# A deformable stage whose sampling products are packed into five matmuls of up to 126 rows

## The chip, the core and the metric

One core of one Trainium2 chip runs the whole program: two layers of a network on 64 images of 1024 channels and 14 by 14 pixels, in fp32. The metric is the device time of one execution in microseconds.

## What is computed

The first layer is a bottleneck of three convolutions (1x1, 3x3, 1x1) with batch norm. The second layer, which the change touches, is a bottleneck whose 3x3 convolution is deformable:

```python
out = relu(group_norm(conv(x, w1)))                  # 1024 -> 256 channels
om = conv(out, w_off, pad=1) + b_off                 # 27 channels
off_x, off_y, mask = om[:, :9], om[:, 9:18], sigmoid(om[:, 18:])
py, px = grid_y + off_y, grid_x + off_x              # a place for each of 9 taps and 196 pixels
sampled = bilinear_sample(out, py, px) * mask        # four corners, zero outside the image
out = relu(group_norm(einsum('bckhw,ock->bohw', sampled, w2)))
out = relu(group_norm(conv(out, w3)) + x)
```

Bilinear sampling is written as a matmul over the 196 source pixels: the sample at (py, px) is the sum over pixels (q, r) of out(q, r) times relu(1 - |py - q|) times relu(1 - |px - r|). The two factors are called hats here, one along y and one along x.

## The kernel before

The first layer takes the first third of the span and is the same in both kernels. The second layer goes over 32 pairs of images. Every product in nearly fp32 precision is three fp32r matmuls (`product3`, lines 69 to 74): high part by high part, and the two mixed terms of high and low.

**Units and tiles.** A pair has nine units of sampling weights: units 0 to 7 are two taps of one image (2 x 196 = 392 columns), unit 8 is the last tap of both images. Each unit serves two tiles of 128 channels, but unit 8 four tiles of 196 columns: 20 tiles a pair (`sample_tile`, line 2015). The 196 source pixels lie on partitions in two halves of 98 = 7 rows of the image by 14 pixels. A tile is therefore 2 halves x 3 terms = 6 matmuls of 98 rows. Its sum is split by ScalarE (`part_v`, high part) and VectorE (`rest_v`, low part, line 1801), and `deform_part` multiplies it by the weights of the taps.

**How a unit is made.** The hats of a pair are made by ScalarE as 126 rows (9 taps x 14 places), the y hats are multiplied by the mask on GpSimd (`mask_hats`, line 1662), and all are stored to DRAM (`store_hats`, line 1321, four DMAs). `load_hats` (lines 1291 to 1314) reads them back, spread over partitions, by three DMAs of 98 rows of 1568 bytes: y hats of the upper seven image rows, each row of the source repeated for 14 partitions; y hats of the lower seven rows likewise; x hats, the 14 rows repeated seven times. The source of each has an outer dimension of 7 and an inner one of 14. GpSimd multiplies y hats by x hats (`make_s`, line 1655), ScalarE takes the high part (`part_s`, line 1438), VectorE the low part (`rest_s`, line 1793). There is a ring of `HATS` = 3 slots; the loads of unit u wait for the low part of unit u - 3 (`s_lo_made`), after which the slot is free.

**What sets the order.** Each engine has one queue, written out by hand as a list of steps in `step`. Work of five pairs is interleaved in it. All loads and stores of hats and the loads of `x1` are issued by SyncE (SP) in one queue; ScalarE's queue issues the loads of `y_in` (line 1364) and the stores of the outputs (line 1354). On SyncE the order of a pair is: loads of units 4 to 8 with the two loads of `x1` among them, the four stores of the next pair's hats, loads of units 0 to 3 of that pair. On GpSimd `mask_hats` of the next pair stands behind `make_s` of unit 8.

**TensorE** runs, for each pair, 20 tiles of `sample_tile`, 36 parts of three matmuls in `deform_part`, 1x1 convolutions (`conv1`, `conv3`, 48 matmuls each), `offsets` (18), three selections (`spread_offsets`, line 1999) and eight transposes of the activations (`transposes`, line 2010).

## Time and profile before

| | us |
|---|---|
| median of three runs | 2997.18 |
| lowest and highest | 2995.97, 2997.70 |
| profiled execution, its own time | 2997.73 |
| its span | 2995.6 |
| first layer and change-over, about | 1000 |
| TensorE busy in the span | 2936.5 (98%) |
| VectorE | 2374.3 (79%) |
| ScalarE | 1798.1 (60%) |
| GpSimd | 717.0 (24%) |

TensorE's clock was granted at full rate in 0.993 of the span. The figures of busy time are averages over stages; what matters below is the steady stretch of the second layer, roughly 1100 to 2900 us. Matmuls overlap their neighbours in the records, so that the distance between two starts, and not the mean duration, is what one costs.

### The profile page before, as it was taken

The numbers are of one execution on the slowest core, as the hardware profiler recorded it, in microseconds if no ns is written. First come the engines' busy times: TensorE is split into PE (matmuls) and PEld (weight loads), VectorE is DVE, ScalarE is ACT, GpSimd is POOL, SyncE is SP. The second block draws the span as 40 slices with busy tenths as digits, with TensorE's granted clock in tenths as the row PEclk, the third lists the DMA queues.
The fourth block names the chain that finished last, engine by engine and source line by source line (L and its number), as shares of the span: only waits on it lengthen the run. The fifth ranks groups of instructions, "written<-read, shape, count | busy, mean of one in ns | idle before, by whom it ended". The sixth has DMA issues, their size and how long they took to land.

```text
span 2995.6 us, 46528 instructions
## 1 busy us (share of the span) xinstructions
PE 2936.5 (98%) x16518; PEld 2861.0 (96%) x16518; DVE 2374.3 (79%) x4872; ACT 1798.1 (60%) x3281; POOL 717.0 (24%) x433
## 2 busy tenths in 40 slices
PE   9999999999998999999999999999999999999997
PEld 9999999999997999999999999999999999999997
DVE  5755888965665688888888888888888888888875
ACT  4544332246654566676666766667666676666664
POOL 0000000000001333333333333333333333333331
PEclk9999999999999999999999999999999999999998
DMA  7774111035653354444444444444444444444431
GB/s 270 217 232 128 44 44 44 22 127 221 256 214 115 119 163 145 145 153 147 157 146 148 155 149 148 151 150 146 155 150 152 152 141 148 148 160 148 143 113 73
DMA packets 209175, 437.34 MB, mean 146 GB/s; under 512 B 18640, under 2 KB 170160, under 8 KB 203312
## 3 DMA queue, kind: packets, MB, share of 16 engines
q1 hardware_dynamic: 159376, 326.77, 32.4%
q10 hardware_dynamic: 49568, 107.60, 11.2%
q8 instruction: 131, 2.15, 0.3%
q14 instruction: 100, 0.82, 0.1%
HBM read 307.66 MB, written 126.64 MB: 145 GB/s over the span
## 4 chain that ended last, share of the span: by engine, by line
PE 58%; DVE 9%; ACT 1%; issue 0%; DMA 0%; POOL 0%; ACTq 0%; DVEq 0%; POOLq 0%
PE work L72 7%; PE work L74 7%; PE sample L72 6%; PE work L73 6%; PE deform L72 6%; PE sample L74 6%; PE sample L73 6%; PE deform L73 6%; PE deform L74 6%; DVE s_lo L1793 2%; DVE x L1817 2%; DVE x_lo L1705 1%; DVE v_lo L1801 1%; DVE x L1699 1%; PE work L2010 1%; PE work L1999 1%
## 5 line engine op out<-in xcount | busy, mean ns | idle before, releaser
L1655 POOL TENSOR_TENSOR hats<-hats 98x784 f32<-98x784 f32 x288 | 602.6, 2092 | 887.2 <-DMA hats<-hat_scratch 857.4
L1447 ACT ACTIVATE v_hi<-sample 128x392 fp32r<-128x392 f32 (+1 forms) x640 | 295.5, 462 | 337.5 <-PE sample L74 318.8
L72 PE MATMUL sample<-s_hi,aT_hi 98*128 98x392 f32 (+1 forms) x1280 | 426.6, 333 | 18.4 <-DVE s_lo L1793 13.5
L73 PE MATMUL sample<-s_lo,aT_hi 98*128 98x392 f32 (+1 forms) x1280 | 419.6, 328 | 0.0
L74 PE MATMUL sample<-s_hi,aT_lo 98*128 98x392 f32 (+1 forms) x1280 | 419.3, 328 | 0.0
L72 PE MATMUL deform<-v_hi,w_w 128*128 128x392 f32 x1152 | 406.4, 353 | 0.9 <-DVE v_lo L1801 0.7
L73 PE MATMUL deform<-v_lo,w_w 128*128 128x392 f32 x1152 | 392.7, 341 | 0.0
L74 PE MATMUL deform<-v_hi,w_w 128*128 128x392 f32 x1152 | 391.6, 340 | 0.0
L1801 DVE TENSOR_TENSOR v_lo<-sample,v_hi 128x392 fp32r<-128x392 f32 (+1 forms) x640 | 327.1, 518 | 74.6 <-ACT v_hi L1447 73.0
L1793 DVE TENSOR_TENSOR s_lo<-hats,s_hi 98x784 fp32r<-98x784 f32 x288 | 346.6, 1204 | 2.6 <-ACT s_hi L1438 1.6
L1438 ACT ACTIVATE s_hi<-hats 98x784 fp32r<-98x784 f32 x288 | 245.6, 853 | 104.3 <-DVE x L1699 77.4
L72 PEld LDWEIGHTS sample<-s_hi,aT_hi 98*128 98x128 f32 x1280 | 241.4, 189 | 34.7 <-DVE s_lo L1793 21.1
L73 PEld LDWEIGHTS sample<-s_lo,aT_hi 98*128 98x128 f32 x1280 | 242.6, 190 | 0.0
L74 PEld LDWEIGHTS sample<-s_hi,aT_lo 98*128 98x128 f32 x1280 | 241.9, 189 | 0.0
L72 PEld LDWEIGHTS deform<-v_hi,w_w 128*128 128x128 f32 x1152 | 217.0, 188 | 8.3 <-issue 5.8
L1817 DVE SCALAR_TENSOR_TENSOR x<-y_home,gn,x 128x196 f32<-128x196 f32 x496 | 220.5, 505 | 0.1
L288 POOL TENSOR_TENSOR bn<-bn,half_neg 128x2 f32<-128x2 f32 (+1 forms) x3 | 3.0, 1012 | 904.8 <-DVE bn L307 622.1
L73 PEld LDWEIGHTS deform<-v_lo,w_w 128*128 128x128 f32 x1152 | 217.4, 189 | 0.0
L74 PEld LDWEIGHTS deform<-v_hi,w_w 128*128 128x128 f32 x1152 | 216.6, 188 | 0.0
L1705 DVE TENSOR_TENSOR x_lo<-x,x_hi 128x392 fp32r<-128x392 f32 x256 | 199.9, 781 | 9.8 <-ACT x_hi L1379 9.8
L1699 DVE SCALAR_TENSOR_TENSOR x<-in_home,scale,x 128x392 f32<-128x392 f32 x248 | 196.2, 792 | 6.2 <-DMA in_home<-y_scratch 6.1
L1503 ACT ACTIVATE x<-x,gn 128x196 f32<-128x196 f32 x496 | 191.6, 448 | 0.7 <-DVE x L1817 0.4
(226 smaller groups left out, 7349.0 us busy)
## 6 DMA issues: line engine op xcount, KB each, us to landing
hats<-hat_scratch SPq DMA_DIRECT2D x768, 150.1 KB
x<-in_x SPq DMA_DIRECT2D x64, 784.0 KB, 5.9
in_home<-y_scratch ACTq DMA_DIRECT2D x248, 196.0 KB, 2.9
out<-x ACTq DMA_DIRECT2D x62, 784.0 KB, 3.4
y_home<-in_x SPq DMA_DIRECT2D x32, 784.0 KB, 5.0
y_scratch<-y_out SPq DMA_DIRECT2D x16, 1568.0 KB, 5.9
terms<-in_x SPq DMA_DIRECT2D x30, 784.0 KB, 4.7
y_scratch<-y_home SPq DMA_DIRECT2D x15, 1568.0 KB, 5.2
```

What stands on the lines that cost most here:

```text
L72: nc.tensor.matmul(out, w_hi, x_hi, start=start, stop=False)
L73: nc.tensor.matmul(out, w_hi, x_lo, start=False, stop=False)
L74: return nc.tensor.matmul(out, w_lo, x_hi, start=False, stop=stop)
L1438: nc.scalar.activation(s_hi[:, unit % 2], hats[:, unit % HATS, 0:2], ACT.Copy).then_inc(s_hi_made, 1)
L1447: nc.scalar.activation(v_hi[:, group % 2, c, 0:taps_of(g), i, :], sample[:, t % 2, 0:cols(g)].rearrange("p (k s) -> p k s", s=PIX), ACT.Co ...
L1503: last = nc.scalar.activation(x1[:, p.buf, i, k, :], x1[:, p.buf, i, k, :], ACT.Relu, bias=gn3.shift[:, i, k:k + 1])
L1655: nc.gpsimd.tensor_tensor(hats[:, slot, 0:2, 0:n], hats[:, slot, 0:2, 0:n], hats[:, slot, 2:3, 0:n].broadcast_to([HALF, 2, n]), ALU.mult). ...
L1699: nc.vector.scalar_tensor_tensor(x1[:, p.buf, :, k, :], from_y, scale[:, k:k + 1], x1[:, p.buf, :, k, :], ALU.mult, ALU.add).then_inc(plus ...
L1705: nc.vector.tensor_tensor(x1_lo[:, k % RING], x1[:, p.buf, :, k, :], x1_hi[:, k % RING].bitcast(F32), ALU.subtract).then_inc(x1_lo_made, 1)
L1793: nc.vector.tensor_tensor(s_lo[:, unit % 2], hats[:, unit % HATS, 0:2], s_hi[:, unit % 2].bitcast(F32), ALU.subtract).then_inc(s_lo_made, 1)
L1801: nc.vector.tensor_tensor(v_lo[:, group % 2, c, 0:taps_of(g), i, :], sample[:, t % 2, 0:cols(g)].rearrange("p (k s) -> p k s", s=PIX), v_h ...
L1817: last = nc.vector.scalar_tensor_tensor(x1[:, p.buf, i, k, :], y[:, i, k, :], gn3.scale[:, i, k:k + 1], x1[:, p.buf, i, k, :], ALU.mult, A ...
```

## The change

**Five products a tile.** The 196 source pixels are split into the upper `UPPER` = 9 image rows (126 pixels) and the lower 5 (70 pixels). The three terms of the upper part are three matmuls of 126 rows. The three terms of the lower part are packed into two matmuls: B, of 112 rows, holds high-by-high and low-by-high of the first four lower rows; C, of 98 rows, holds high-by-low of all five and the two remaining terms of the last row. The first three products of a tile read only what ScalarE makes, and the low part of the weights is waited for in front of the fourth.

**Three planes of hats.** For that a unit has three y planes of 126 rows (A, B, C) and an x plane. `load_hats` issues six DMAs in place of three: A (source dimensions 9 by 14), B as 56 rows (4 by 14) and 70 rows (5 by 14), C as 70 rows (5 by 14) and 56 rows (one row repeated), x (9 by 14). Unit 8 takes twelve in place of six. `make_s` multiplies 3 x 392 elements on 126 partitions in place of 2 x 392 on 98. `part_s` has a second instruction of 392 elements, with row masks. High and low parts are written into the slot itself, and the high part of plane A into one of two further planes; the ring has 4 slots, and the loads of unit u wait for the last tile of unit u - 4 (`sampled`).

**Activations.** There are twelve transposes a pair in place of eight, in three groups, from `a_f` and from a copy of its lower rows that a new step `copy_rows` on ScalarE makes. `part_aT` has three instructions of 256 columns in place of one of 512, `rest_aT` two in place of one.

**Elsewhere.** `conv1`, `conv3` and `deform_part` keep their three terms, but both products with the high operand come first, and the low operand is waited for behind them. Three semaphores of the first layer are used again. The mask lies in a free slot of `x1_lo`. The selectors have 96 rows in place of 64. The lists of steps of all engines but SyncE's (where one load of `x1` moves up by two units) are rearranged.

SyncE, from the load of `x1` that precedes unit 8 to the loads of unit 0 of the next pair. Before (`hats` is the slot, `hat_scratch` the stored hats, `offs_b` the hats as made):

```order
L1301 DMA hats<-hat_scratch 98x1x196 [waits s_lo_made]
L1301 DMA hats<-hat_scratch 98x1x196
L1304 DMA hats<-hat_scratch 98x1x196
L1301 DMA hats<-hat_scratch 98x1x196 x2
L1304 DMA hats<-hat_scratch 98x1x196
L1284 DMA x<-in_x 128x1568 [waits w3b_lo_made]
L1321 DMA hat_scratch<-offs_b 9x14x196 [waits hat_made] x2
L1321 DMA hat_scratch<-offs_b 9x14x196 [waits masked] x2
L1309 DMA hats<-hat_scratch 98x1x392 [waits hats_stored0,s_lo_made]
L1309 DMA hats<-hat_scratch 98x1x392
L1312 DMA hats<-hat_scratch 98x1x392
```

And now, from the middle of unit 8:

```order
L1352 DMA hats_f<-hat_scratch 126x1x196
L1325 DMA x1<-in_x 128x1568 [waits w3b_lo_made]
L1360 DMA hat_scratch<-offs_b 9x14x196 [waits hat_made] x2
L1360 DMA hat_scratch<-offs_b 9x14x196 [waits masked] x2
L1348 DMA hats_f<-hat_scratch 126x1x392 [waits hats_stored0,sampled]
L1348 DMA hats_f<-hat_scratch 56x1x392
L1348 DMA hats_f<-hat_scratch 70x1x392 x2
L1350 DMA hats_f<-hat_scratch 56x392
L1352 DMA hats_f<-hat_scratch 126x1x392
```

The stores keep their place; a unit's loads are six where there were three, and their first waits for tiles, not for the low part of an earlier unit.

GpSimd, from unit 6 of one pair over the mask to the first units of the next. Before:

```order
L1655 TENSOR_TENSOR hats<-hats 98x784 [waits hats_loaded0,gn1_done]
L1655 TENSOR_TENSOR hats<-hats 98x784 [waits hats_loaded1]
L1655 TENSOR_TENSOR hats<-hats 98x784 [waits hats_loaded2]
L1662 TENSOR_TENSOR offs_b<-offs_b 126x392 [waits mask_made,hat_made]
L1129 TENSOR_TENSOR gn<-gn,half_neg 128x2 [waits gn3_done]
L1655 TENSOR_TENSOR hats<-hats 98x784 [waits hats_loaded0,gn3_done]
```

And now:

```order
L1717 TENSOR_TENSOR hats_f<-hats_f 126x1176 [waits first_loaded0,gn1_done]
L1717 TENSOR_TENSOR hats_f<-hats_f 126x1176 [waits hats_loaded0]
L1717 TENSOR_TENSOR hats_f<-hats_f 126x1176 [waits hats_loaded1]
L1724 TENSOR_TENSOR offs_b<-offs_b,x_lo_f 126x392 [waits mask_made,hat_made]
L1144 TENSOR_TENSOR gn<-gn,half_neg 128x2 [waits gn3_done]
L1717 TENSOR_TENSOR hats_f<-hats_f 126x1176 [waits hats_loaded2,gn3_done]
```

The order is the same: the mask of the next pair still stands behind unit 8's multiplication. The instructions are longer.

The diff, cut to what the text speaks of:

```diff
 ONE = 29
 LATE = ("gn1_scale", "gn1_bias", "gn2_scale", "gn2_bias", "gn3_scale", "gn3_bias")
-HATS = 3
+HATS = 4
+UPPER = 9
+LOWER = SIDE - UPPER
+A_ROWS = UPPER * SIDE
+B_ROWS = 2 * (LOWER - 1) * SIDE
+C_ROWS = (LOWER + 2) * SIDE
 RING = 3
 BUFS = 4
...
-                slot, n = unit % HATS, 2 * PIX
-                at_least(sp, s_lo_made, unit - HATS + 1)
+                first, loaded = plane_of(unit), hats_loaded[unit % HATS]
+                if unit >= HATS:
+                    sp.wait_ge(sampled, tiles_until(unit - HATS))
                 if u < 2:
                     sp.wait_ge(hats_stored[i], 32 * (p.n + 1))
-                t0 = 2 * g * PIX
+                parts = [(i, slice(0, 2 * PIX))]
                 if u == UNITS - 1:
...
-                for half in range(2):
-                    src = hats_at[p.n % 2, 0, i, half * ROWS:(half + 1) * ROWS, t0:t0 + n]
-                    sp.dma_start(hats[:, slot, half, 0:n], src.unsqueeze(1).broadcast_to([ROWS, SIDE, n])
-                                 ).then_inc(hats_loaded[slot], 16)
-                src = hats_at[p.n % 2, 1, i, :, t0:t0 + n]
-                sp.dma_start(hats[:, slot, 2, 0:n], src.unsqueeze(0).broadcast_to([ROWS, SIDE, n])
-                             ).then_inc(hats_loaded[slot], 16)
+                    parts = [(i, slice(i * PIX, (i + 1) * PIX)) for i in range(2)]
+                for i, at in parts:
+                    n = at.stop - at.start
+                    y_hat, x_hat = (hats_at[p.n % 2, e, i, :, 2 * g * PIX:2 * g * PIX + n] for e in range(2))
+                    to = planes_f[:, first:first + 4, at]
+                    b_rows = B_ROWS // 2
+                    for dst, rows in ((to[:, 0], slice(0, UPPER)), (to[0:b_rows, 1], slice(UPPER, SIDE - 1)),
+                                      (to[b_rows:A_ROWS, 1], slice(UPPER, SIDE)),
+                                      (to[0:LOWER * SIDE, 2], slice(UPPER, SIDE))):
+                        sp.dma_start(dst, y_hat[rows].unsqueeze(1).broadcast_to([rows.stop - rows.start, SIDE, n])
+                                     ).then_inc(loaded, 16)
+                    sp.dma_start(to[LOWER * SIDE:A_ROWS, 2], y_hat[SIDE - 1:SIDE].broadcast_to([A_ROWS - LOWER * SIDE, n])
+                                 ).then_inc(loaded, 16)
+                    sp.dma_start(to[:, 3], x_hat.unsqueeze(0).broadcast_to([UPPER, SIDE, n])).then_inc(loaded, 16)
             @of_pair
...
             @of_pair
             def part_aT(p, i):
-                act.wait_ge(transposed, 2 * p.n + i + 1)
+                act.wait_ge(transposed, 3 * p.n + i + 2)
                 at_least(act, sampled, TILES * (p.n - 1) + (TILES - 2 if i == 0 else TILES))
-                nc.scalar.activation(aT_hi[:, i].rearrange("p h c -> p (h c)"), work[0:HALF, 2 * i, :],
-                                     ACT.Copy).then_inc(aT_hi_made, 1)
+                nc.scalar.activation(aT[:, i, 0], work[0:A_ROWS, 2 * i, 0:CMID], ACT.Copy)
+                nc.scalar.activation(aT[:, i, 2], work[0:A_ROWS, 2 * i, CMID:2 * CMID], ACT.Relu,
+                                     scale=consts["row_masks"][0:A_ROWS, 0:1])
+                nc.scalar.activation(aT[0:C_ROWS, i, 3], work[0:C_ROWS, 1, i * CMID:(i + 1) * CMID], ACT.Relu,
+                                     scale=consts["row_masks"][0:C_ROWS, 1:2]).then_inc(aT_hi_made, 1)
             @of_pair
             def part_s(p, u):
                 unit = UNITS * p.n + u
+                first = plane_of(unit)
                 act.wait_ge(s_made, unit + 1)
                 at_least(act, sampled, tiles_until(unit - 2))
-                nc.scalar.activation(s_hi[:, unit % 2], hats[:, unit % HATS, 0:2],
+                nc.scalar.activation(planes[:, unit % 2:first + 2:first + 1 - unit % 2], planes_f[:, first:first + 2],
                                      ACT.Copy).then_inc(s_hi_made, 1)
+                nc.scalar.activation(planes[:, first + 3], planes_f[:, first + 2], ACT.Relu,
+                                     scale=consts["row_masks"][0:A_ROWS, 2:3]).then_inc(c_made, 1)
...
             @of_pair
             def make_s(p, u):
                 unit = UNITS * p.n + u
-                n, slot = 2 * PIX, unit % HATS
-                pool.wait_ge(hats_loaded[slot], 48 * (unit // HATS + 1 + (p.n + u // (UNITS - 1) if slot == HATS - 1 else 0)))
-                nc.gpsimd.tensor_tensor(hats[:, slot, 0:2, 0:n], hats[:, slot, 0:2, 0:n],
-                                        hats[:, slot, 2:3, 0:n].broadcast_to([HALF, 2, n]), ALU.mult).then_inc(s_made, 1)
+                first = plane_of(unit)
+                pool.wait_ge(hats_loaded[unit % HATS], loads_until(unit))
+                s = planes_f[:, first:first + 3]
+                nc.gpsimd.tensor_tensor(s, s, planes_f[:, first + 3:first + 4].broadcast_to([A_ROWS, 3, 2 * PIX]),
+                                        ALU.mult).then_inc(s_made, 1)
             @of_pair
             def mask_hats(p):
                 pool.wait_ge(hat_made, p.n + 1)
...
-                nc.vector.tensor_tensor(aT_lo[:, i].rearrange("p h c -> p (h c)"), work[0:HALF, 2 * i, :],
-                                        aT_hi[:, i].rearrange("p h c -> p (h c)").bitcast(F32),
-                                        ALU.subtract).then_inc(aT_lo_made, 1)
+                nc.vector.tensor_tensor(aT[:, i, 1:3], work[0:A_ROWS, 2 * i, :].rearrange("p (e c) -> p e c", e=2),
+                                        aT[:, i, 0:3:2].bitcast(F32), ALU.subtract)
+                nc.vector.tensor_tensor(aT[0:C_ROWS, i, 3], work[0:C_ROWS, 1, i * CMID:(i + 1) * CMID],
+                                        aT[0:C_ROWS, i, 3].bitcast(F32), ALU.subtract).then_inc(aT_lo_made, 1)
             @of_pair
             def rest_s(p, u):
                 unit = UNITS * p.n + u
-                dve.wait_ge(s_hi_made, unit + 1)
-                nc.vector.tensor_tensor(s_lo[:, unit % 2], hats[:, unit % HATS, 0:2],
-                                        s_hi[:, unit % 2].bitcast(F32), ALU.subtract).then_inc(s_lo_made, 1)
+                first = plane_of(unit)
+                dve.wait_ge(c_made, c_before + unit + 1)
+                nc.vector.tensor_tensor(planes[:, first:first + 3:2], planes_f[:, first:first + 3:2],
+                                        planes[:, unit % 2:first + 4:first + 3 - unit % 2].bitcast(F32),
+                                        ALU.subtract).then_inc(s_lo_made, 1)
             @of_pair
...
             @of_pair
             def transposes(p, i):
                 if i == 0:
                     pe.wait_ge(mask_made, p.n + 1)
+                elif i == 1:
+                    at_least(pe, y_written, KX * (p.n - 2) + KX - 1)
                 else:
-                    at_least(pe, y_written, KX * (p.n - 2) + KX - 1)
-                for h in range(2):
-                    for k in range(KM):
-                        last = nc.tensor.transpose(work[0:HALF, 2 * i, (h * KM + k) * P:(h * KM + k + 1) * P],
-                                                   a_f[:, k, i, h * HALF:(h + 1) * HALF], ident[:])
+                    at_least(pe, y_written, KX * (p.n - 1))
+                pe.wait_ge(rows_copied, copies_before + p.n + 1)
+                for k in range(KM):
+                    if i < 2:
+                        nc.tensor.transpose(work[0:A_ROWS, 2 * i, k * P:(k + 1) * P], a_f[:, k, i, 0:A_ROWS], ident[:])
+                        last = nc.tensor.transpose(work[0:A_ROWS, 2 * i, CMID + k * P:CMID + (k + 1) * P],
+                                                   lower[:, 2 * k + i, 0:A_ROWS], ident[:])
+                    else:
+                        for image in range(2):
+                            last = nc.tensor.transpose(work[0:C_ROWS, 1, image * CMID + k * P:image * CMID + (k + 1) * P],
+                                                       lower[:, 2 * k + image, copies - C_ROWS:], ident[:])
                 last.then_inc(transposed, 1)
...
                 u, n = min(t // 2, UNITS - 1), cols(g)
                 at = i * PIX if u == UNITS - 1 else 0
                 unit = UNITS * p.n + u
+                first = plane_of(unit)
                 if t in (0, 2):
                     pe.wait_ge(aT_lo_made, 2 * p.n + i + 1)
                 if c == 0:
+                    pe.wait_ge(s_hi_made, unit + 1)
+                at_least(pe, v_lo_made, TILES * p.n + t - 1)
+                to, a_part = sample[:, t % 2, 0:n], aT[:, i, :, c * P:(c + 1) * P]
+                high, parts = planes[:, unit % 2, at:at + n], planes[:, first:first + 3, at:at + n]
+                nc.tensor.matmul(to, a_part[:, 0], high, start=True, stop=False)
+                nc.tensor.matmul(to, a_part[:, 1], high, start=False, stop=False)
+                nc.tensor.matmul(to, a_part[0:B_ROWS, 2], parts[0:B_ROWS, 1], start=False, stop=False)
+                if c == 0:
                     pe.wait_ge(s_lo_made, unit + 1)
-                at_least(pe, v_lo_made, TILES * p.n + t - 1)
-                for h in range(2):
-                    last = product3(nc, sample[:, t % 2, 0:n], aT_hi[:, i, h, c * P:(c + 1) * P],
-                                    aT_lo[:, i, h, c * P:(c + 1) * P],
-                                    s_hi[:, unit % 2, h, at:at + n], s_lo[:, unit % 2, h, at:at + n],
-                                    start=(h == 0), stop=(h == 1))
+                nc.tensor.matmul(to, a_part[:, 0], parts[:, 0], start=False, stop=False)
+                last = nc.tensor.matmul(to, a_part[0:C_ROWS, 3], parts[0:C_ROWS, 2], start=False, stop=True)
                 last.then_inc(sampled, 1)
...
                 if t == 0:
-                    pe.wait_ge(v_lo_made, TILES * p.n + 4 * g + 3 + k)
+                    pe.wait_ge(v_hi_made, TILES * p.n + 4 * g + 3 + k)
                 if part == 0 and g == 0:
                     at_least(pe, b_raw, p.n)
                 for tap in range(taps_of(g)):
...
+                if t == 0:
+                    pe.wait_ge(v_lo_made, TILES * p.n + 4 * g + 3 + k)
+                for tap in range(taps_of(g)):
```

## Rows read from the trace of the kernel before

**Rows 1.** Window: busy us of each engine (instructions), clock, DMA share, GB/s
```profile
1200.00:2800.00 1600.00, 1587.49 (x9131) 1549.50 (x9131) 1380.23 (x3122) 1101.13 (x2242) 568.09 (x331) 1.00 0.46 150
```

**Rows 2.** SyncE's line 1321: min/median/max ns, first and last start
```profile
L1321 SPq DMA_DIRECT2D hat_scratch<-offs_b x116: 735/752/811, 1123.4 to 2888.9; - x116
```

**Rows 3.** Timeline of TensorE: start, us, what, count
```profile
2002.34 0.33 PE L1999 MATMUL sums_ps<-x_hi,select_s 64*126 64x392 f32 x1
2002.60 0.44 PE L72 MATMUL sample<-s_hi,aT_hi 98*128 98x392 f32 x1
...
2011.89 0.34 PE L74 MATMUL sample<-s_hi,aT_lo 98*128 98x392 f32 x1
2012.07 0.60 PE L2010 MATMUL work<-ident_s,in_home 128*98 128x128 f32 x4
2012.42 0.43 PE L72 MATMUL deform<-v_hi,w_w 128*128 128x392 f32 x1
...
2017.66 0.28 PE L73 MATMUL sample<-s_lo,aT_hi 98*128 98x196 f32 x1
2017.78 0.28 PE L74 MATMUL sample<-s_hi,aT_lo 98*128 98x196 f32 x1
```

**Rows 4.** Groups by form, 1050 to 2950 us: count, busy, mean, idle
```profile
L1655 POOL TENSOR_TENSOR hats<-hats 98x784 f32<-98x784 f32 x272 | 568.7, 2091 | 834.0 <-DMA hats<-hat_scratch 805.6 <-DVE gn L1155 28.4
...
L1793 DVE TENSOR_TENSOR s_lo<-hats,s_hi 98x784 fp32r<-98x784 f32 x274 | 331.1, 1208 | 2.4 <-ACT s_hi L1438 1.4
...
L1705 DVE TENSOR_TENSOR x_lo<-x,x_hi 128x392 fp32r<-128x392 f32 x232 | 183.5, 791 | 4.9 <-ACT x_hi L1379 4.9
...
L1379 ACT ACTIVATE x_hi<-x 128x392 fp32r<-128x392 f32 x232 | 123.5, 532 | 22.9 <-PE work L74 16.4
```

**Rows 5.** Timelines of VectorE and, below, GpSimd, one stretch
```profile
2040.66 0.56 DVE L1705 TENSOR_TENSOR x_lo<-x,x_hi 128x392 fp32r<-128x392 f32 x1
2041.38 2.02 DVE L1705 TENSOR_TENSOR x_lo<-x,x_hi 128x392 fp32r<-128x392 f32 x1 [0.17 <-ACT x_hi L1379]
...
2040.85 2.12 POOL L1655 TENSOR_TENSOR hats<-hats 98x784 f32<-98x784 f32 x1 [0.71 <-DVE gn L1155]
```

**Rows 6.** Timeline of SyncE's queue: the stores, one unit's loads
```profile
2004.64 3.16 SPq L1321 DMA_DIRECT2D hat_scratch<-offs_b  x4
2009.14 1.54 SPq L1309 DMA_DIRECT2D hats<-hat_scratch  x2
2010.73 0.73 SPq L1312 DMA_DIRECT2D hats<-hat_scratch  x1
```

**Rows 7.** Timeline of GpSimd from unit 8 to unit 2
```profile
2002.39 2.37 POOL L1655 TENSOR_TENSOR hats<-hats 98x784 f32<-98x784 f32 x1 [4.95 <-DMA hats<-hat_scratch]
2005.14 1.04 POOL L1662 TENSOR_TENSOR offs_b<-offs_b 126x392 f32<-126x392 f32 x1 [0.38 <-ACT offs_b L1423]
...
2015.11 1.88 POOL L1655 TENSOR_TENSOR hats<-hats 98x784 f32<-98x784 f32 x1 [7.00 <-DMA hats<-hat_scratch]
2018.40 1.89 POOL L1655 TENSOR_TENSOR hats<-hats 98x784 f32<-98x784 f32 x1 [1.40 <-DMA hats<-hat_scratch]
2021.83 2.24 POOL L1655 TENSOR_TENSOR hats<-hats 98x784 f32<-98x784 f32 x1 [1.54 <-DMA hats<-hat_scratch]
```

**Rows 8.** Windows moving loads of planes, and, last, an output
```profile
2012.10:2013.40 1.30, 1.30 (x11) 1.30 (x9) 1.30 (x4) 1.30 (x4) 0.00 (x0) 1.00 0.45 123
2034.60:2036.60 2.00, 2.00 (x13) 2.00 (x13) 1.93 (x10) 1.53 (x3) 1.48 (x1) 1.00 0.99 393
```

**Rows 9.** DMA issues of the page: count, KB each, median us to landing
```profile
hats<-hat_scratch SPq DMA_DIRECT2D x768, 150.1 KB
x<-in_x SPq DMA_DIRECT2D x64, 784.0 KB, 5.9
...
out<-x ACTq DMA_DIRECT2D x62, 784.0 KB, 3.4
```

**Rows 10.** Waits of SyncE's queue: total us, times, longest
```profile
SPq L1309 <- DVE s_lo L1793: 830.8, 162, 9.6
```

434 lines of the change are left out of this document (235 added, 199 removed).

## The prediction, made before the changed kernel was run

> **What bounds the kernel now.** I read the windows first. In a stretch of 1600 us of the second layer TensorE is busy 1587.5 us, 99.2%, at full clock, VectorE 86.3%, ScalarE 69%, GpSimd 36%, and the DMA engines 46% on the mean [rows 1]. So TensorE sets the time there. The period of a pair: line 1321 issues four stores a pair, 116 of them are 29 pairs, so 28 periods lie between the first and the last group, (2888.9 - 1123.4 - 2.4) / 28 = 63.0 us [rows 2]. A matmul of 392 columns starts 0.18 us after its neighbour, one of 196 columns 0.12 us, and four transposes take 0.35 us [rows 3].
>
> A mean of 46% for 16 DMA engines hides how they are used. In a window in which only hats are loaded the share is 0.45, at 123 GB/s; when an output of 784 KB leaves, it is 0.99 at 393 GB/s [rows 8]. 0.45 is 7 of 16. Each load of 98 rows has an outer source dimension of 7: it seems to be cut into as many pieces as that dimension, one engine each. And SyncE issues the three loads of a unit in 2.3 us [rows 6], while GpSimd gets units 0, 1 and 2 of a pair 3.3 and 3.4 us apart, waiting for DMA each time [rows 7]. Several loads are then in flight at once, and still only seven engines work: they are the same seven. Each carries 3 x 14 = 42 packets of 1568 bytes a unit, at 3.36 / 42 = 80 ns. Before the change that costs nothing: SyncE waits 831 us in all, 26 us a pair, for free slots [rows 10].
>
> **What the change removes on TensorE.** Per pair 16 matmuls of 392 columns (16 x 0.18 = 2.9 us) and 4 of 196 (0.5). It adds four transposes (0.35). The selections of 64 rows start 0.26 us before their successor and not 0.18 [rows 3]; with 96 rows that may go, 0 to 0.5 us a pair, and I take 0.2. Sum: -3.2 us, a period of 59.8 if TensorE stays the bound, with 0 to 0.3 us more for the third group of transposes. The new order of high and low products removes waits that TensorE hardly has (it idles 0.8%), so nothing for it.
>
> **ScalarE** gets nine more instructions of 392 elements, 9 x 0.53 = 4.8 us [rows 4], and some 2 us for the copies and the activations in four pieces (estimated from the same row): 43.4 + 7 = 50 us of 59.8. It stays behind TensorE's pace. Nothing for it.
>
> **GpSimd and VectorE.** A multiplication of 784 elements takes 1.88 us, one of 392 (the mask) 1.04 [rows 7]: 0.84 us per 392 elements, so 2.72 us for 1176. Nine a pair are 24.5 us, hidden by themselves. But VectorE stands still behind them: a subtraction that takes 0.56 us takes 2.02 when it starts 0.5 us into a multiplication, and ends 0.4 us after it [rows 5]. The means show how often: 791 ns for that line, 1208 for `rest_s` [rows 4]. In the other direction a multiplication that starts behind such an instruction is lengthened, 2.37 for 1.88 [rows 7]. Per pair VectorE is busy 0.863 x 63.0 = 54.3 us. The change adds 0.7 us (`rest_aT`) and, of the 9 x 0.84 = 7.6 us by which multiplications grow, between nothing and all. With half of it, because about half of the nine meet a two-operand instruction, 58.8 us: full, if the period is 59.8.
>
> **The loads.** Here the change is largest. A unit now needs six DMAs with 126 + 56 + 70 + 70 + 56 + 126 = 504 rows in place of 294. Their outer dimensions are 9, 4, 5, 5, 56 (one row repeated) and 9. If each is cut as before, into the largest number of equal pieces up to 16, they use 9, 4, 5, 5, 14 and 9 engines, with 14 packets on each used engine, but 4 for the one repeated row. If all begin at the same engine, as the three loads of before do, the first four engines carry 5 x 14 + 4 = 74 packets a unit, against 42. At 80 ns that is 5.92 us a unit. The lower end of a packet's price comes from the output: 393 GB/s over 16 engines at 0.99 is 24.8 GB/s for one, 63 ns for 1568 bytes, 4.7 us a unit. I take 80 ns, because it was measured on these very loads.
>
> The Trainium skill (DMA: Bandwidth & Descriptors, section on why a DMA increments its semaphore by 16) states this cut: the largest k up to 16 that divides the slowest dimension of both sides, on the lowest-numbered k engines. By that rule the stack on the first four is as I count it, and the time is that of the forecast; the 0.45 of the window agrees for k = 7. No row shows where a transfer on four or five engines begins.
>
> **The loop that closes over them.** SyncE, the DMA engines and GpSimd form a loop of their own: unit 8's loads, its multiplication, then the mask of the next pair, which stands behind it on GpSimd, then the stores, then the loads of unit 0, and so on to unit 8. Added up for the changed kernel:
> - multiplication of unit 8 to the start of the mask: 2.8 us (2.72, and no wait for ScalarE);
> - start of the mask to the issue of the first load: 2005.14 to 2009.14, 4.0 us [rows 6, 7], unchanged;
> - that issue to GpSimd's start on unit 0: 2009.14 to 2015.11, 5.97, and 5.92 - 3.36 = 2.56 more: 8.5;
> - units 1 to 7: 7 x 5.92 = 41.4;
> - unit 8: twelve DMAs at 0.73 us of issue are 8.8 us, by bytes it is a unit of 5.9: 7, nearer to the bytes as SyncE runs ahead;
> - one load of `x1` in the same queue, 784 KB at 393 GB/s: 2.0; the two outputs of equal size on the other queue and the same engines [rows 8, 9]: 4.0, of which some 0.7 fall into the two pauses at the top.
>
> Together 69.0 us. The second load of `x1` lies in the pause for the mask; the loads of `y_in` are inside the measured 3.36. The low end: 63 ns a packet gives 6.8 + 7.3 + 7 x 4.7 + 5.9 + 2.0 + 4.0 = 58.9, and the eight loads of `y_in`, 196 KB each, come back with 4.2: 63.1. The high end takes unit 8 by issue and no overlap: 71.5 us. All of it lies above TensorE's 59.8. The waits for slots don't change this: the tiles of unit u - 4 are done long before load u comes to the head of a queue that is late. So what was hidden under 26 us of slack becomes the bound, and TensorE waits for the high parts of a unit, mostly around unit 0 and unit 8.
>
> **Forecast:** 69.0 in place of 63.0 for 31 periods, +186 us. The profiled execution took 2997.7 us (its span is 2995.6), within 1 us of the median of the three runs: 2998 + 186 = 3184 us.
>
> **Rivals.**
> - *The loads spread, TensorE stays the bound.* If the transfers on few engines begin at different ones, even over nine engines, a unit is 56 packets, 4.5 us, the loop 6.8 + 7.1 + 31.4 + 7 + 2 + 4 = 58.3 us, and the period TensorE's 59.8: 2998 - 31 x 3.2 = 2899 us, faster. It decides below about 60 packets on the fullest engine. For it: no row shows loads of different cuts side by side. Against: three loads in flight kept to seven engines.
> - *VectorE becomes the bound.* The loads spread, but the longer multiplications lock out more than half of the time: 54.3 + 0.7 + 7.6 = 62.6 us and waits that can't be hidden. 62.5 to 64 a pair, 2980 to 3030 us. The Trainium skill (GPSIMD Engine Reference, Specifications) says that the engine's SBUF interfaces are shared with VectorE for instructions with two SBUF inputs; [rows 5] agree with 1.46 us of standing still. That alone would give this rival's time.
> - *The change does less than it says*: six matmuls stay six. The written order has five a tile, so no chance worth a number.
>
> **How the numbers follow.** Loads stacked on the first engines and the loop the bound: 0.78. Spread, TensorE the bound: 0.13. VectorE the bound: 0.06, half of it within 0.2% of before or below, half above. The rest, 0.03, is shared. About 0.2% (6 us) is what a measurement can tell from no change. Faster 0.15, same 0.03, slower 0.82. The first case alone spans 3001 (63.1 a pair) to 3262 (71.5). The range goes from 2990, which takes in part of VectorE's case, to 3280, since outputs and loads may also meet worse than in the window; left out is the case of TensorE.
>
> **What would show it.** TensorE busy under 92% in the second layer; a store group every 66 to 71 us; GpSimd's multiplications about 2.7 us and, for units 1 to 7, some 5.9 us apart, each waiting for DMA; SyncE's wait for slots small; a share of the DMA engines well below one in windows of loads, near 5 of 16, at under 120 GB/s. VectorE's share falls. The forecast is wrong if multiplications of successive units can follow within 4.5 us, or if SyncE's queue still waits over 10 us a pair for tiles while TensorE is at 99%.

## The result, and the profile of the changed kernel

The changed kernel takes 3264.8 us, the median of four runs (3250.4 to 3267.5), against 2996.6 us (2992.7 to 2997.7) for the kernel before: a ratio of 1.089, 95% interval 1.087 to 1.090. The forecast was 3184 us in a range from 2990 to 3280, slower with a chance of 0.82. Direction and range held; the time is 81 us above the forecast, and the experiments show that a cause which I gave a chance of 0.06 has the larger part in it. The profiled execution took 3267.5 us, its span is 3265.4.

Three lines of the profile of the changed kernel: busy time of the engines; the granted clock in 40 slices, in tenths; and the chain of work that ended last, followed back from the last instruction, as shares of the span (SPq is time in SyncE's queue, `issue` is time in which an engine waited for nothing that the profile shows):

```profile
PE 2979.2 (91%) x16006; PEld 2848.5 (87%) x16006; DVE 2588.5 (79%) x4936; ACT 1991.8 (61%) x3761; POOL 923.5 (28%) x433
...
PEclk9999999999988999999999999999999999999998
...
PE 33%; DVE 23%; DMA 4%; ACT 4%; issue 3%; SPq 2%; POOL 2%; ACTq 0%; POOLq 0%; DVEq 0%
```

The window that answers to [rows 1], a stretch of 1700 us of the second layer. The busy times are, in order, those of TensorE, its weight loads, VectorE, ScalarE and GpSimd:

```profile
1300.00:3000.00 1700.00, 1526.18 (x8227) 1446.49 (x8226) 1472.85 (x2997) 1181.39 (x2470) 688.57 (x312) 0.96 0.57 175
```

TensorE falls from 99% to 90% busy, at a mean clock of 0.96 and not 1.00. The stores of the planes, which answer to [rows 2], give the period: (3143.5 - 1157.2 - 2.4) / 28 = 70.85 us in place of 63.0.

```profile
L1360 SPq DMA_DIRECT2D hat_scratch<-offs_b x116: 744/761/784, 1157.2 to 3143.5; - x116
```

So a pair of images costs 7.85 us more. Split by TensorE: it idles (1700 - 1526.2) / 1700 x 70.85 = 7.2 us of a pair, where it idled 0.5 before; up to 2.8 us (0.04 of 70.85) go into matmuls at a lower clock, less by what of the low clock falls into idle time; what is left is at least 61 us, against 62.5 before. VectorE's busy time is 0.866 x 70.85 = 61.4 us a pair, where it was 54.3.

GpSimd in the changed kernel from unit 8 of one pair to unit 4 of the next, which answers to [rows 7] (start, duration, what; in brackets the idle time before it and what ended it):

```profile
2005.21 2.72 POOL L1717 TENSOR_TENSOR hats_f<-hats_f 126x1176 f32<-126x1176 f32 x1 [3.07 <-DMA hats_f<-hat_scratch]
2007.88 1.02 POOL L1724 TENSOR_TENSOR offs_b<-offs_b,x_lo_f 126x392 f32<-126x392 f32 x1
...
2020.61 2.75 POOL L1717 TENSOR_TENSOR hats_f<-hats_f 126x1176 f32<-126x1176 f32 x1 [9.23 <-DMA hats_f<-hat_scratch]
2025.90 2.75 POOL L1717 TENSOR_TENSOR hats_f<-hats_f 126x1176 f32<-126x1176 f32 x1 [2.54 <-DMA hats_f<-hat_scratch]
2032.14 2.89 POOL L1717 TENSOR_TENSOR hats_f<-hats_f 126x1176 f32<-126x1176 f32 x1 [3.50 <-DMA hats_f<-hat_scratch]
2036.94 2.68 POOL L1717 TENSOR_TENSOR hats_f<-hats_f 126x1176 f32<-126x1176 f32 x1 [1.91 <-DMA hats_f<-hat_scratch]
...
2043.26 2.85 POOL L1717 TENSOR_TENSOR hats_f<-hats_f 126x1176 f32<-126x1176 f32 x1 [0.85 <-DMA hats_f<-hat_scratch]
```

Each multiplication takes 2.7 to 2.9 us and waits for DMA, and units 0 to 4 of this pair are 5.66 us apart on the mean. That is close to the forecast. The whole pair is not so even: over 23 pairs of the trace unit 0 starts 16.5 us after unit 8, units 1 to 3 follow 5.4 us apart, units 4 to 6 9.3, unit 7 after 4.8 and unit 8 after 5.7. And SyncE's queue, which answers to [rows 10], still waits for free slots, 505 / 32 = 15.8 us a pair, nearly all of it in front of the loads of units 3 to 6.

```profile
SPq L1348 <- PE sample L2114: 505.3, 168, 12.1
```

And VectorE stands behind GpSimd in a place that the forecast did not look at. VectorE and, below, TensorE of the changed kernel in one stretch:

```profile
2005.69 2.30 DVE L1125 TENSOR_TENSOR gn<-gn 128x32 f32<-128x32 f32 x1
2008.02 0.92 DVE L1128 SCALAR_TENSOR_TENSOR gn<-gn 128x32 f32<-128x32 f32 x1
2008.87 0.18 DVE L1131 TENSOR_REDUCE gn<-gn 128x2 f32<-128x32 f32 x1
...
2009.32 0.35 PE L1138 MATMUL sums_ps<-gn,ones_s 128*128 128x4 f32 x2 [2.01 <-DVE gn L1133]
2009.53 0.76 PE L2090 MATMUL work<-ident_s,x_lo_f 128*98 128x128 f32 x4
...
2010.74 0.53 PE L90 MATMUL deform<-v_hi,w_w 128*128 128x392 f32 x1
2011.06 0.53 PE L91 MATMUL deform<-v_hi,w_w 128*128 128x392 f32 x1
```

L1125, in the function that reduces the statistics of a GroupNorm, squares 32 numbers a partition. It begins 0.5 us into the multiplication of 2005.21 and ends 0.1 us after it: 2.30 us. The next one is held up by the multiplication of the mask. TensorE waits 2.0 us for the sums, and its matmuls of 392 columns then start 0.33 us apart and not 0.18: the granted clock has fallen to the lower of its two levels, 1.2 GHz, for some 3.5 us: 0.59 on the mean of the 4.2 us below.

```profile
2005.00:2009.30 4.30, 2.30 (x14) 1.78 (x13) 4.23 (x8) 3.23 (x7) 3.68 (x2) 1.00 0.50 165
2009.30:2013.50 4.20, 4.18 (x17) 4.20 (x18) 3.96 (x12) 1.16 (x2) 1.03 (x1) 0.59 0.46 115
2013.50:2016.00 2.50, 2.50 (x16) 2.46 (x16) 2.50 (x8) 1.21 (x3) 0.00 (x0) 1.00 0.59 160
```

In these windows (columns as in [rows 1]) the clock is 1.00, then 0.59, then 1.00 again. The wait for the sums is the largest that TensorE has in the changed kernel (us in all, times, longest):

```profile
PE sums_ps L1138 <- DVE gn L1133: 113.0, 72, 3.4
```

### The profile page after: what moved, and what is told of

It reads as the page before. It is cut to its first block, busy times and chain, and to the rows that moved or that the text cites. A ratio compares the mean times of both kernels' runs of the same rounds, so it can differ in the third digit from the quotient of the medians.

```text
span 3265.4 us, 47194 instructions
## 1 busy us (share of the span) xinstructions
PE 2979.2 (91%) x16006; PEld 2848.5 (87%) x16006; DVE 2588.5 (79%) x4936; ACT 1991.8 (61%) x3761; POOL 923.5 (28%) x433
## 4 chain that ended last, share of the span: by engine, by line
PE 33%; DVE 23%; DMA 4%; ACT 4%; issue 3%; SPq 2%; POOL 2%; ACTq 0%; POOLq 0%; DVEq 0%
PE deform L90 4%; PE deform L95 4%; PE deform L91 4%; DMA hats_f<-hat_scratch 4%; DVE x_lo L1771 4%; DVE gn L1125 3%; DVE x L1886 3%; PE work L95 3%; PE work L90 2%; DVE v_lo L1870 2%; PE work L91 2%; PE sample L2108 2%; DVE x L1761 2%; PE sample L2113 2%; SPq L1348 2%
## 5 line engine op out<-in xcount | busy, mean ns | idle before, releaser
L1717 POOL TENSOR_TENSOR hats_f<-hats_f 126x1176 f32<-126x1176 f32 x288 | 811.4, 2817 | 1145.6 <-DMA hats_f<-hat_scratch 1144.9
L90 PE MATMUL deform<-v_hi,w_w 128*128 128x392 f32 x1152 | 423.6, 368 | 0.6 <-ACT v_hi L1506 0.6
L91 PE MATMUL deform<-v_hi,w_w 128*128 128x392 f32 x1152 | 414.1, 359 | 0.0
L1861 DVE TENSOR_TENSOR hats<-hats_f,hats 126x784 fp32r<-126x784 f32 x288 | 325.1, 1137 | 90.8 <-ACT hats L1497 89.3
L95 PE MATMUL deform<-v_lo,w_w 128*128 128x392 f32 x1152 | 329.7, 360 | 1.2
L1495 ACT ACTIVATE hats<-hats_f 126x784 fp32r<-126x784 f32 x288 | 246.7, 857 | 121.4 <-POOL hats_f L1717 96.6
L2108 PE MATMUL sample<-hats,aT 126*128 126x392 f32 (+1 forms) x640 | 223.0, 348 | 57.3 <-DVE v_lo L1870 56.0
L1409 ACT ACTIVATE x<-x,shift 128x392 f32<-128x392 f32 x256 | 157.5, 615 | 147.9 <-DVE x L1761 147.7
L90 PEld LDWEIGHTS deform<-v_hi,w_w 128*128 128x128 f32 x1152 | 233.4, 203 | 1.3 <-ACT v_hi L1506 0.9
L91 PEld LDWEIGHTS deform<-v_hi,w_w 128*128 128x128 f32 x1152 | 233.7, 203 | 0.0
L2113 PE MATMUL sample<-hats,aT 126*128 126x392 f32 (+1 forms) x640 | 220.2, 344 | 7.0 <-DVE hats L1861 6.4
L2110 PE MATMUL sample<-hats,aT 112*128 112x392 f32 (+1 forms) x640 | 216.5, 338 | 0.0
L2109 PE MATMUL sample<-hats,aT 126*128 126x392 f32 (+1 forms) x640 | 216.4, 338 | 0.0
L2114 PE MATMUL sample<-hats,aT 98*128 98x392 f32 (+1 forms) x640 | 216.3, 338 | 0.0
```

The costliest lines, as they stand in the source:

```text
L90: nc.tensor.matmul(out, w_hi, x_hi, start=start, stop=False)
L91: nc.tensor.matmul(out, w_lo, x_hi, start=False, stop=False)
L95: return nc.tensor.matmul(out, w_hi, x_lo, start=False, stop=stop)
L1717: nc.gpsimd.tensor_tensor(s, s, planes_f[:, first + 3:first + 4].broadcast_to([A_ROWS, 3, 2 * PIX]), ALU.mult).then_inc(s_made, 1)
L1861: nc.vector.tensor_tensor(planes[:, first:first + 3:2], planes_f[:, first:first + 3:2], planes[:, unit % 2:first + 4:first + 3 - unit % 2] ...
L2108: nc.tensor.matmul(to, a_part[:, 0], high, start=True, stop=False)
```

## The experiments

Twelve kernels have a time. (A thirteenth, an earlier form of experiment 8 with a separate multiplication of 392 elements ahead of each unit's own, needed more SBUF than there is and has none.) Two names recur in the expectations. **L** is the theory of the forecast: the loads of a unit are stacked on the first DMA engines and pace the pair. **V** is the rival: VectorE is locked out while GpSimd multiplies. To take either away, work is left out or data fetched in another order, so most of these kernels compute wrong samples; each expectation says which. The kernel before took 2995 to 2998 us beside each of them; "period" is worked out from the stores as above.

**1. The changed kernel with spread loads.** The source of each load is read with its 14 positions outermost, so that the load can be cut 14 ways.

```diff
-  y_hat[rows].unsqueeze(1).broadcast_to([rows.stop - rows.start, SIDE, n])
+  y_hat[rows].unsqueeze(0).broadcast_to([SIDE, rows.stop - rows.start, n])
-  x_hat.unsqueeze(0).broadcast_to([UPPER, SIDE, n])
+  x_hat[0:UPPER].unsqueeze(0).broadcast_to([SIDE, UPPER, n])
```

> The changed kernel with one edit: the source rows of each load are read in another order (14 repeats outside, image rows inside), so that the hats land on wrong partitions and the output is not the reference's. Count of DMAs, bytes, waits and all other work stay. The outer source dimension becomes 14 everywhere, so each load should be cut over 14 engines: 9 + 4 + 5 + 5 + 4 + 9 = 36 packets a unit on the fullest engine in place of 74. Theory L (stacked loads close the loop): units can follow within 3.5 us, the period falls from 70.9 to 60 to 62 us, 2900 to 2970 us in all. Theory V (VectorE is locked out by the longer multiplications on GpSimd, whatever the loads do): hardly any change, 3200 to 3265 us. Between them: both take part.

Measured: 3211.8 us, ratio 1.072 (1.068 to 1.076), period 69.7 us. Only 53 us are gone. This was V's number; as the sole cause, the theory of the forecast was out by 240 us or more.

**2. The changed kernel with short multiplications.** GpSimd multiplies one plane of three.

```diff
-  s = planes_f[:, first:first + 3]
-  nc.gpsimd.tensor_tensor(s, s, planes_f[:, first + 3:first + 4].broadcast_to([A_ROWS, 3, 2 * PIX]),
+  s = planes_f[:, first:first + 1]
+  nc.gpsimd.tensor_tensor(s, s, planes_f[:, first + 3:first + 4],
```

> The changed kernel with one edit: GpSimd multiplies plane A only, 392 elements in about 1.04 us, in place of three planes in 2.8 us; planes B and C stay unmultiplied, so the output is not the reference's. Loads untouched. Theory L: only the 1.7 us of unit 8's multiplication leave the loop, 31 x 1.7 = 53 us: 3210 us. Theory V: VectorE loses most of what it stands still, some 8 us or more a pair, and the time falls to about 3000 us.

Measured: 3073.8 us, ratio 1.026 (1.023 to 1.029), period 65.1 us: 191 us are gone, with the loads left as they are. But V's 3000 is not reached either. The edit takes away two things at once: VectorE's wait, and 1.7 us between a unit's landing and its high part, which alone would give the 53 us of theory L. That most of the 191 us is the first is argued from the chains: GpSimd itself has 2% of the changed kernel's, VectorE 23%. Here the chain shows what now comes last, SyncE's queue and the transfers, with 5% for VectorE:

```profile
PE 27%; SPq 16%; DMA 13%; DVE 5%; ACT 4%; issue 3%; POOL 2%; ACTq 0%; POOLq 0%; DVEq 0%
```

**3. The kernel before with stacked loads.** Its x hats are fetched by a load whose outer dimension is 2, so that two engines carry 14 + 14 + 49 = 77 packets a unit.

```diff
-  src.unsqueeze(0).broadcast_to([ROWS, SIDE, n])
+  src[0:1].unsqueeze(0).broadcast_to([2, HALF // 2, n])
```

> The kernel before with one edit: the load of the x hats reads one row repeated with an outer dimension of 2 in place of 7, so it runs on two engines with 49 packets each; with the 28 of the two other loads the two fullest engines carry 77 packets a unit in place of 42. Bytes, count of DMAs and all else stay; the x hats are wrong, so the output is not the reference's. Theory L: units follow 77 x 80 ns = 6.2 us apart, the loop is about 70 us a pair, 3200 us in all, as in the changed kernel. Theory V: 2997 us, as GpSimd's and VectorE's work is that of before.

Measured: 3251.5 us, ratio 1.085 (1.082 to 1.089), period 71.0 us. Nothing else was changed, so stacking is real and alone costs the kernel before 255 us, 50 more than L's 3200. Its chain and its largest wait of SyncE:

```profile
DMA 25%; PE 13%; DVE 11%; POOL 9%; issue 7%; SPq 4%; ACT 3%; ACTq 0%; POOLq 0%; DVEq 0%
```
```profile
SPq L1309 <- DVE s_lo L1793: 924.7, 188, 10.3
```

SyncE waits 29 us a pair for slots here, more than in the kernel before [rows 10], and the time is still up by 8.5%. A long wait for slots does not show that loads have room to spare: with three slots, a load that takes longer from issue to landing holds back the unit, its tiles, and by them the next slot. That order of events is argued; the transfers' 25% of the chain, where the kernel before has 0%, is measured.

**4. The kernel before with five matmuls a tile.** One product of the lower rows is left out.

```diff
-  for h in range(2):
-      last = product3(nc, sample[:, t % 2, 0:n], aT_hi[:, i, h, ...], aT_lo[:, i, h, ...], s_hi[...], s_lo[...], ...)
+  product3(nc, to, aT_hi[:, i, 0, ...], aT_lo[:, i, 0, ...], s_hi[..., 0, ...], s_lo[..., 0, ...], start=True, stop=False)
+  nc.tensor.matmul(to, aT_hi[:, i, 1, ...], tap_high, start=False, stop=False)
+  last = nc.tensor.matmul(to, aT_lo[:, i, 1, ...], tap_high, start=False, stop=True)
```

> The kernel before with one product of each tile left out (the high-by-low term of the lower half), five matmuls of 98 rows in place of six; the output is not the reference's. It is the packing's gain on TensorE alone, with loads, GpSimd and VectorE as before. Prediction's term: 16 x 0.18 + 4 x 0.12 = 3.4 us a pair, 32 pairs, 2997 - 108 = 2890 us. If VectorE (86% busy) already limits once TensorE gets faster, less: 2930 us or more.

Measured: 2938.3 us, ratio 0.981 (0.974 to 0.988), period 61.0 us. TensorE's gain comes through by 58 us only, the expectation's second case (2930 us or more). The two runs lie 18 us apart, and by the interval it is 36 to 79 us. VectorE is 90% busy and TensorE no longer full:

```profile
1300.00:2700.00 1400.00, 1371.23 (x7790) 1323.13 (x7790) 1261.53 (x2829) 988.00 (x2021) 516.01 (x298) 1.00 0.48 154
```

**5. Spread loads and short multiplications together** in the changed kernel (both diffs above).

> The changed kernel with both edits at once: every load of hats takes its source rows in another order, so that its outer dimension is 14 (36 packets of a unit on the fullest engine in place of 74), and GpSimd multiplies only the first of the three planes (about 1.0 us in place of 2.8). The samples are wrong. Alone, the first edit took off 53 us and the second 191. If stacked loads (L) and VectorE locked behind GpSimd (V) are together the whole cost, each hiding part of the other, this comes near TensorE's pace of the forecast: 2900 to 2960 us. If the two are separate, they add up: 3265 - 53 - 191 = 3021 us. Above 3030 a third cost is left, such as the issue of six DMAs a unit on SyncE (4.3 us of issue a unit) or a worse order on TensorE itself.

Measured: 3026.6 us, ratio 1.009 (1.005 to 1.014), period 63.4 us. The two gains add up nearly in full (3265 - 53 - 191 = 3021), and a third cost is left. SyncE's queue, with 16% of the chain, points to it: in this stretch the DMAs of a unit follow one another without a gap, and one unit takes from 2000.45 to 2005.24, 4.8 us.

```profile
2000.45 3.31 SPq L1348 DMA_DIRECT2D hats_f<-hat_scratch  x4
2003.80 0.55 SPq L1350 DMA_DIRECT2D hats_f<-hat_scratch  x1
2004.39 0.80 SPq L1352 DMA_DIRECT2D hats_f<-hat_scratch  x1
2005.24 3.23 SPq L1348 DMA_DIRECT2D hats_f<-hat_scratch  x4
```

**6. and 7. The same two edits in the kernel before**, as controls. Short multiplications (one plane of two):

> The kernel before, GpSimd multiplying one of the two planes only (about 1.0 us in place of 2.0; the samples are wrong). TensorE is 99% busy in it, so both theories expect little: 2975 to 2998 us. VectorE's busy time a pair falls from 54.3 to about 50 us. If it fell well below 2975, the lock cost something in the kernel before too.

Measured: 2975.4 us, ratio 0.992 (0.989 to 0.994), at the lower edge of what was expected. The period is 62.2 us and TensorE has no idle time left at all:

```profile
1300.00:2700.00 1400.00, 1400.00 (x8084) 1371.65 (x8083) 1111.85 (x2765) 967.66 (x1977) 327.44 (x293) 1.00 0.47 152
```

So the lock cost the kernel before some 22 us too. Spread loads:

> The kernel before, its three loads of a unit with source rows in the order of outer dimension 14 (21 packets of a unit on the fullest engine in place of 42; the samples are wrong). It is the control for the edit of the same kind in the changed kernel. Both theories expect no change, since TensorE is the bound and SyncE waits 26 us a pair for free slots: 2990 to 3003 us, with a share of the DMA engines in windows of loads alone near 14 of 16 while they last.

Measured: 3000.0 us, ratio 1.000 (0.998 to 1.002): nothing, as expected, though the edit acts: on the mean of 23 pairs units 1 and 2 follow after 3.4 and 2.0 us, where it was 4.0 and 3.0. The expected share near 14 of 16 did not show: in four windows of 1 us over these loads it is 0.38 to 0.65. SyncE takes about 2.5 us to issue a unit, in which 294 packets at 80 ns would fill 0.6 of 16 engines (an estimate).

**8. The kernel before with longer multiplications**, three planes in place of two.

```diff
-  nc.gpsimd.tensor_tensor(hats[:, slot, 0:2, 0:n], hats[:, slot, 0:2, 0:n],
-                          hats[:, slot, 2:3, 0:n].broadcast_to([HALF, 2, n]), ALU.mult)
+  nc.gpsimd.tensor_tensor(hats[:, slot, 0:3, 0:n], hats[:, slot, 0:3, 0:n],
+                          hats[:, slot, 2:3, 0:n].broadcast_to([HALF, 3, n]), ALU.mult)
```

> The kernel before, with GpSimd's multiplication of a unit over three planes in place of two (98 x 1176 elements; the third, which nobody reads afterwards, is the x hat times itself), so about 2.8 us in place of 2.0, as in the changed kernel. Loads, matmuls and order stay as before, and all that is computed for the output too. V (VectorE locked behind GpSimd): its busy time a pair rises from 54.3 to 59 to 62 us and small operations are held up: 3030 to 3150 us. L (loads): GpSimd is idle 64% and VectorE has 14% to spare, so nothing: 2997 to 3010 us.

Measured: 3112.8 us, ratio 1.039 (1.026 to 1.053), period 66.7 us. One engine that is idle for 64% of the time [rows 1] got 0.7 us more a unit, and the kernel is 118 us slower. This is V with the loads as they were. GpSimd, which passes each unit on 0.7 us later, has none of the chain; VectorE has 18%, where it had 9%:

```profile
PE 47%; DVE 18%; ACT 3%; DMA 2%; issue 1%; POOL 0%; ACTq 0%; DVEq 0%; POOLq 0%
```

VectorE's busy time is 0.880 x 66.7 = 58.7 us a pair, 4.4 more than in the kernel before:

```profile
1300.00:2700.00 1400.00, 1346.83 (x7535) 1291.15 (x7534) 1232.45 (x2582) 911.31 (x1848) 594.44 (x273) 0.99 0.43 141
```
```profile
L1655 POOL TENSOR_TENSOR hats<-hats 98x1176 f32<-98x1176 f32 x288 | 795.2, 2762 | 805.4 <-DMA hats<-hat_scratch 767.7
```

**9. The changed kernel with four spread loads a unit.** Experiment 1, and the planes of the lower rows come in one load of 126 rows each:

```diff
-  for dst, rows in ((to[:, 0], slice(0, UPPER)), (to[0:b_rows, 1], slice(UPPER, SIDE - 1)),
-                    (to[b_rows:A_ROWS, 1], slice(UPPER, SIDE)),
-                    (to[0:LOWER * SIDE, 2], slice(UPPER, SIDE))):
+  for dst, rows in ((to[:, 0], slice(0, UPPER)), (to[:, 1], slice(0, UPPER)),
+                    (to[:, 2], slice(0, UPPER))):
...
-  sp.dma_start(to[LOWER * SIDE:A_ROWS, 2], y_hat[SIDE - 1:SIDE].broadcast_to([A_ROWS - LOWER * SIDE, n])
-               ).then_inc(loaded, 16)
```

> The changed kernel with four loads a unit in place of six, each of 126 rows with an outer dimension of 14: 36 packets of a unit on the fullest engine and some 3.3 us of issue on SyncE in place of 4.9. GpSimd multiplies three planes as in the changed kernel. The samples are wrong. What is left beside TensorE's own work is V alone. V, with the price that taking it away had (191 us of the changed kernel): 3080 to 3180 us. If issue was the larger part of what remained in the run with spread loads (3212): under 3050 us. It also bounds what any better cut of the loads could give with this GpSimd work: it beats the kernel before only under 2997.

Measured: 3294.2 us, ratio 1.100 (1.081 to 1.119), period 72.2 us. Neither case was right: with faster loads the kernel is *slower* than with six of them. GpSimd and VectorE in one stretch, and TensorE's first matmul after it:

```profile
2030.37 8.37 POOL L1714 TENSOR_TENSOR hats_f<-hats_f 126x1176 f32<-126x1176 f32 x3 [9.65 <-DMA hats_f<-hat_scratch]
...
2030.61 5.61 DVE L1883 SCALAR_TENSOR_TENSOR x<-y_home,gn,x 128x196 f32<-128x196 f32 x2
2036.14 3.02 DVE L1758 SCALAR_TENSOR_TENSOR x<-in_home,scale,x 128x392 f32<-128x392 f32 x1
2039.08 0.35 DVE L1867 TENSOR_TENSOR v_lo<-sample,v_hi 128x196 fp32r<-128x196 f32 x1
...
2039.58 0.51 PE L2105 MATMUL sample<-hats,aT 126*128 126x196 f32 x1 [7.22 <-DVE v_lo L1867]
```

Three units have landed, and GpSimd multiplies them back to back for 8.4 us. In that time VectorE gets three short additions through, one for each multiplication, which take 1.4 us (2 x 0.41 + 0.61) when nothing is in their way. TensorE stands still for 7.2 us, and then its clock is down for another 5 us or so (busy time of each engine, clock, DMA share and GB/s in steps of 5 us):

```profile
2030.00:2035.00 5.00, 2.35 (x17) 2.02 (x16) 5.00 (x4) 3.50 (x10) 4.63 (x2) 1.00 0.75 235
2035.00:2040.00 5.00, 0.42 (x2) 0.46 (x3) 5.00 (x5) 0.00 (x0) 3.74 (x2) 0.55 0.01 3
2040.00:2045.00 5.00, 5.00 (x20) 5.00 (x20) 2.50 (x6) 2.65 (x6) 0.00 (x0) 0.50 0.15 40
2045.00:2050.00 5.00, 5.00 (x27) 5.00 (x27) 3.37 (x8) 3.66 (x9) 0.00 (x0) 0.93 0.54 158
```

The clock in these rows is 1.00, 0.55, 0.50 and 0.93. Over the whole run it is 0.955 in a span of 3305.4 us. With six spread loads (experiment 1) it is 0.976 in 3214.1 us. At most 0.045 x 3305 = 149 us are lost to the clock here and 0.024 x 3214 = 77 us there, so this one effect can hold most of the 82 us between them. Nor was this stretch the only one. TensorE's wait for the low parts of the samples at the start of a tile, first here and then with six spread loads (us in all, times, longest):

```profile
PE sample L2105 <- DVE v_lo L1867: 191.6, 44, 7.3
PE sample L2108 <- DVE v_lo L1870: 49.6, 36, 4.5
```

VectorE's busy time a pair is the same in both, about 61.5 us; what differs is when it is held up. It looks as if slower loads keep the multiplications apart and so shelter it.

**10. The same with short multiplications.**

> The same, and GpSimd multiplies the first plane only. All three costs are gone: stacked packets, long multiplications, issue of six DMAs. If they are the whole, TensorE is the bound with the packed matmuls: 2880 to 2940 us, a store group every 59.8 to 61 us, SyncE waiting for slots again. If it stays near the 3027 us of six spread loads and short multiplications, issue was not the third cost, and something in the new order or in the matmuls themselves is.

Measured: 2956.5 us, ratio 0.987 (0.983 to 0.991), period 61.3 us. All three costs gone, the kernel is faster than the one before, and TensorE nearly full at full clock:

```profile
1300.00:2700.00 1400.00, 1376.10 (x7841) 1323.11 (x7840) 1136.40 (x2855) 1124.20 (x2357) 319.02 (x297) 1.00 0.65 202
```

TensorE's busy time is 0.983 x 61.3 = 60.3 us a pair; the forecast had 59.8 for it. With 1.0 us of idle time the period is 1.5 us over it, and the time is 16 us above the expected range. SyncE's queue has 0% of the chain, where it had 16% in experiment 5. Whether the two DMAs cost by their issue or by their landing was not separated.

**11. Five matmuls a tile and short multiplications in the kernel before** (the edits of 4 and 6).

> The kernel before with five matmuls a tile in place of six (one product of the lower rows left out) and GpSimd multiplying one plane of two. The samples are wrong. With five matmuls alone it took 2938 us, 50 us above TensorE's price of 2890, with VectorE at 90%. If the lock behind GpSimd is what kept back these 50 us: 2885 to 2905 us. If not (waits in the written order): 2920 to 2940 us.

Measured: 2870.3 us, ratio 0.958 (0.954 to 0.963), period 58.9 us, TensorE 100% busy. Against the kernel with short multiplications alone (2975.4) the fifth of six matmuls is worth 105 us; the rows of [rows 3] had said (16 x 0.18 + 4 x 0.12) x 31 = 104. With the long ones it was worth 58; the rest is what the longer multiplications had kept back. The time is 15 us below the expected range, which left out the 22 us that short multiplications give with six matmuls too (experiment 6).

**12. The changed kernel, the multiplication of a unit in three instructions.** All is computed as in the changed kernel.

```diff
-  s = planes_f[:, first:first + 3]
-  nc.gpsimd.tensor_tensor(s, s, planes_f[:, first + 3:first + 4].broadcast_to([A_ROWS, 3, 2 * PIX]),
-                          ALU.mult).then_inc(s_made, 1)
+  for e in range(3):
+      s, x_hat = (planes_f[:, first + r, 0:2 * PIX] for r in (e, 3))
+      last = nc.gpsimd.tensor_tensor(s, s, x_hat, ALU.mult)
+  last.then_inc(s_made, 1)
```

> The changed kernel, GpSimd's multiplication of a unit (1176 elements a partition, 2.8 us) cut into three of 392, one for each plane; all is computed as before. If VectorE waits for the end of the GpSimd instruction that runs (E), a wait is at most 1.0 us instead of 2.8: 3080 to 3170 us, although GpSimd works some 0.3 to 0.5 us longer a unit. If the whole of GpSimd's work keeps it out (W): 3265 to 3290 us.

Measured: 3210.5 us, ratio 1.072 (1.068 to 1.076), period 69.1 us. The time lies between the two expectations, and the trace tells why. Rows of VectorE in the changed kernel (first four) and with three instructions (last four): count, then busy us and mean ns.

```profile
L1771 DVE TENSOR_TENSOR x_lo<-x,x_hi 128x392 fp32r<-128x392 f32 x256 | 228.5, 896 | 24.2 <-ACT x_hi L1418 24.2
L1761 DVE SCALAR_TENSOR_TENSOR x<-in_home,scale,x 128x392 f32<-128x392 f32 x248 | 210.9, 851 | 8.8 <-DMA in_home<-y_scratch 8.4 <-issue 0.3
L1886 DVE SCALAR_TENSOR_TENSOR x<-y_home,gn,x 128x196 f32<-128x196 f32 x496 | 240.2, 541 | 1.1
L1125 DVE TENSOR_TENSOR gn<-gn 128x8 f32<-128x8 f32 (+1 forms) x96 | 136.1, 1418 | 3.3
```
```profile
L1773 DVE TENSOR_TENSOR x_lo<-x,x_hi 128x392 fp32r<-128x392 f32 x256 | 160.1, 626 | 30.5 <-ACT x_hi L1418 30.5
L1763 DVE SCALAR_TENSOR_TENSOR x<-in_home,scale,x 128x392 f32<-128x392 f32 x248 | 174.8, 705 | 8.6 <-DMA in_home<-y_scratch 8.2 <-issue 0.3
L1888 DVE SCALAR_TENSOR_TENSOR x<-y_home,gn,x 128x196 f32<-128x196 f32 x496 | 201.4, 463 | 1.1
L1125 DVE TENSOR_TENSOR gn<-gn 128x8 f32<-128x8 f32 (+1 forms) x96 | 55.6, 579 | 3.3
```

Every operation with two operands in SBUF became shorter, and VectorE's busy time fell from 61.4 to 0.783 x 69.1 = 54.1 us a pair. What VectorE waits for is the end of the GpSimd instruction that runs, and the length of one instruction sets the price. That part of the expectation held. But GpSimd pays: a unit in three instructions takes 3.0 us when VectorE is quiet and up to 4.7 us when it is not, the high parts come later (ScalarE waits 200 us for GpSimd over the run, 97 us in the changed kernel), and the chain now goes through transfers, SyncE's queue and GpSimd:

```profile
PE 24%; DVE 12%; SPq 11%; DMA 11%; POOL 5%; ACT 5%; issue 3%; ACTq 0%; POOLq 0%; DVEq 0%
```
```profile
2023.48 4.71 POOL L1719 TENSOR_TENSOR hats_f<-hats_f 126x392 f32<-126x392 f32 x3 [4.06 <-DMA hats_f<-hat_scratch]
```

No kernel that computes all of the reference beat the one before. Its own multiplication in two instructions, for which experiments 6 and 12 speak, was not run.

## Why the prediction was right in sign and range, and wrong in its cause

- **TensorE's own term** (-3.2 us a pair) was right for the matmuls: they alone gave 105 us where 104 were counted (experiments 6 and 11). The net term was too large. TensorE fills 62.2 us a pair in the kernel before with short multiplications (experiment 6) and 60.3 in the packed one (experiment 10): -1.9. The missing 1.3 us were not traced; matmuls of 392 columns start 0.18 us apart in both.
- **ScalarE at nothing**: right as far as shown. It is 0.69 x 70.85 = 49 us a pair busy, where 50 was expected, and where nothing else is in the way (experiment 10) TensorE is 98% busy.
- **Units 5.92 us apart, the first multiplication 8.5 us after the first load's issue**: measured 5.66 and 9.1 in the stretch shown, with 5.4 for units 1 to 3 over 23 pairs. Multiplications never followed within 4.5 us there. How the loads are cut and stacked was read rightly from a mean share of 7 in 16, and experiment 3 shows that such a stack alone costs 255 us in the kernel before. But the sign "near 5 of 16, at under 120 GB/s" did not show. Where hats alone are loaded it is 7 of 16 (0.44) at 148 GB/s, and the forecast's own 504 packets in 5.92 us are already 133 GB/s:

```profile
2024.00:2025.50 1.50, 0.67 (x5) 0.37 (x4) 1.25 (x4) 1.50 (x6) 0.00 (x0) 1.00 0.44 148
```

- **The sum of the loop is where the argument failed.** It said that the loads run without a wait for slots and so set 69.0 us. But the changed kernel waits 15.8 us a pair for slots, where I had named a small wait as a sign of the forecast. (The sign against it asked for over 10 us with TensorE at 99%; TensorE is at 90%.) So the measured 70.85 us is not that loop alone: units 4 to 6 lie 9.3 us apart, and the loads that wait for tiles are those of units 3 to 6. That the tiles are late because of VectorE as well is argued from experiments 2 and 8. That sum and result lie 3% apart is luck for the most part. The loads' share, taken away first, is 53 us, and with short multiplications 47.
- **VectorE's term was mis-sized**, and with it the rival's chance. I took half of 7.6 us, 4.5 us with `rest_aT`, for a busy time of 58.8. It is 61.4, 7.1 more than before, so its share did not fall as I had said it would (86.3% and 86.6%). 3.9 us of these are one small operation: three a pair went from a mean of 189 ns (L1110 before) to 1490 ns in the steady stretch (L1125 now, 1418 over the whole run, experiment 12). I had costed the long subtractions and not looked at which operations lie where multiplications now run. Worse was the step behind it: I took VectorE as harmless while its busy time stays under the period. Experiment 8 has it at 88% and costs 118 us. A lock doesn't only fill an engine, it comes in one piece at a moment when TensorE waits for the result, and then TensorE's clock falls as well. I had put nothing for the clock; it is up to 2.8 us a pair. L1110 in the kernel before:

```profile
L1110 DVE TENSOR_TENSOR gn<-gn 128x8 f32<-128x8 f32 (+1 forms) x96 | 18.1, 189 | 3.3
```

- **What the rival got wrong.** V alone, 2980 to 3030 us, assumed that spread loads go with it. Spread loads with the long multiplications gave 3212 (experiment 1). It too was only counted as busy time.
- **A cost that was in the sum in passing**: six issues a unit, 0.73 us each. I used it for unit 8 only. With loads spread and multiplications short it decides: four in place of six give 3027 - 2956 = 70 us.

Put in a row, from the changed kernel: short multiplications -191 us, spread loads -47, two DMAs fewer a unit -70, and one is 40 us below the kernel before. In another order the steps have other sizes, down to the opposite sign: without short multiplications, the two fewer DMAs cost 82 us. Why the loop of loads and the locked VectorE add up nearly in full, although each can hide the other, was not settled.

## What to carry to other kernels

Before giving GpSimd a longer two-operand instruction, list what VectorE does with two SBUF operands in the same stretch, small operations on the way to a matmul first; price each at the length of one GpSimd instruction, and don't count on VectorE's mean share. When several things pace a loop, remove each alone and then together before naming a cause: a faster transfer can bunch up the work behind it and lose time. And a queue that still waits for slots doesn't show that its transfers are free.

## What the runs showed of the hardware beyond what I expected

- VectorE with two operands in SBUF waits for the end of the running GpSimd instruction, and beside back-to-back ones one got through for each of them: 8.4 us for three short additions. A subtraction with one operand in PSUM is not touched: `v_lo` has a mean of 519 ns in the changed kernel and 518 in the kernel before.
- It acts both ways. Three GpSimd instructions of 392 elements take 3.0 us undisturbed and up to 4.7 beside a busy VectorE.
- After TensorE had idled 2.0 us, matmuls ran at half the clock for about 3.5 us, and after 7.2 us for at least 5. In the changed kernel this adds up to 2.8 us a pair to the 7.2 us for which it idles.
- An issue on SyncE's queue costs 0.65 to 0.77 us where the source's outer dimension is 4 to 9 (changed kernel, medians), and 0.78 to 0.80 with 14 (experiment 1). Spreading a load is not free on the issuing side.
